# Second attention and expert half of a transformer block: new instruction orders, chunk 0 normalised by VectorE, group scores from pair sums, SP's tables ahead of the weights

## The reference

```
x = x + xattn0(LN(x), ctx)        # one head, softmax over 32 keys; out = (LN(x) + attended) @ Wo.T + bo
x = x + ffn0(LN(x))               # router, 8 experts, the best one per token; gelu MLP 128-256-128, times its gate
x = x + xattn1(LN(x), ctx, mask)  # 16 heads of width 8, 32 keys
x = x + ffn1(LN(x))               # 16 experts of width 96, top 4 of 16 out of the 2 best of 4 groups, plus a shared expert
```

```
scores = sigmoid(LN(x) @ gate_w.T);  sb = scores + gate_bias
group_scores = sum(top_2 of the 4 sb in each group)      # 4 groups of 4 experts
keep the 2 best groups; tidx = top_4 of the kept sb
w = scores[tidx] / (sum + 1e-20) * 2.5
y = sum over experts of combine[:, e] * (silu(g_e) * u_e) @ w2_e;   out = y + shared
```

## Time and profile before

| | us |
|---|---|
| median of three runs | 311.48 (310.99 to 311.97) |
| the profiled execution | 313.38 |
| its span, first to last instruction | 311.6 |
| TensorE busy in the span | 264.1 (85%) |
| VectorE busy | 191.7 (62%) |
| ScalarE busy | 162.9 (52%) |
| GpSimd busy | 155.4 (50%) |
| mean granted TensorE clock | 0.919 of full |

### The profile page before, as it was taken

How to read it: one execution, slowest core, us unless ns; L and a number is a source line. 1 busy time by engine, 2 the same in 40 slices (tenths; PEclk the granted TensorE clock), 3 DMA queues, 4 the chain that set the end, 5 groups by cost and what they waited for, 6 DMA issues and landing times. The chain is left out here.

```text
span 311.6 us, 4963 instructions
## 1 busy us (share of the span) xinstructions
PE 264.1 (85%) x1542; PEld 193.6 (62%) x1542; DVE 191.7 (62%) x577; ACT 162.9 (52%) x324; POOL 155.4 (50%) x182
## 2 busy tenths in 40 slices
PE   8899962259989287979899987999899989899993
PEld 7689852249984042444468645875477867687871
DVE  5555557014441348666975998689976599665561
ACT  2946330485641034157488654878457745455541
POOL 6722577439402888251176151743178535565561
PEclk9996655559999969999999999999999999999998
DMA  7960013447841111000000000000000000000000
GB/s 239 405 236 1 18 35 101 119 127 191 241 130 37 51 35 34 8 2 0 2 0 2 1 0 1 2 0 14 23 1 0 2 34 1 1 2 34 0 0 34
DMA packets 15372, 16.86 MB, mean 54 GB/s; under 512 B 2147, under 2 KB 13011, under 8 KB 15091
## 3 DMA queue, kind: packets, MB, share of 16 engines
q1 hardware_dynamic: 9520, 11.65, 11.8%
q10 hardware_dynamic: 4802, 2.80, 2.9%
q0 software_dynamic: 1024, 2.10, 2.4%
HBM read 11.96 MB, written 4.59 MB: 53 GB/s over the span
## 5 line engine op out<-in xcount | busy, mean ns | idle before, releaser
L854 POOL TENSOR_TENSOR lring<-hm,hring 128x512 fp32r<-128x512 f32 (+1 forms) x52 | 67.9, 1307 | 77.6 <-ACT hring L746 76.3
L740 ACT ACTIVATE act<-bank 128x512 f32<-128x512 f32 (+1 forms) x52 | 31.0, 597 | 38.5 <-PE bank L1166 38.3
L1143 DVE TENSOR_TENSOR act<-act,bank 128x512 f32<-128x512 f32 x48 | 32.9, 685 | 27.0 <-PE bank L1166 25.7
L1166 PE MATMUL bank<-xTh,gu1h 128*128 128x512 f32 (+1 forms) x104 | 43.6, 419 | 2.6 <-DVE hm L1154 1.7
L1166 PE MATMUL bank<-xTh,gu1l 128*128 128x512 f32 (+1 forms) x104 | 41.1, 395 | 0.0
L1166 PE MATMUL bank<-xTl,gu1h 128*128 128x512 f32 (+1 forms) x104 | 40.8, 393 | 0.0
L581 ACT ACTIVATE xn<-x,shift_of,rstd 128x128 f32<-128x128 f32 x64 | 26.4, 483 | 26.4 <-POOL shift_of L775 26.3
L1154 DVE TENSOR_TENSOR hm<-act,bank 128x512 f32<-128x512 f32 (+1 forms) x52 | 35.6, 685 | 7.4 <-PE bank L1166 4.9
L746 ACT CAST hring<-hm 128x512 fp32r<-128x512 f32 (+1 forms) x52 | 32.1, 618 | 12.4 <-DVE hm L1154 11.4
L1166 PEld LDWEIGHTS bank<-xTh,gu1h 128*128 128x128 f32 (+1 forms) x104 | 19.3, 186 | 14.8 <-DVE act L1143 3.6
L788 POOL DMA_INDIRECT xn<-sorted_y,home x16 | 15.7, 983 | 21.2 <-DMA sorted_y<-ys 17.3
(11 more groups left out here) (217 smaller groups left out, 521.0 us busy)
## 6 DMA issues: line engine op xcount, KB each, us to landing
w<-in_w SPq DMA_DIRECT2D x23, 129.0 KB, 2.4
wf<-in_gu SPq DMA_DIRECT2D x1, 1632.0 KB, 14.2
xs<-sorted_x SPq DMA_DIRECT2D x23, 64.0 KB, 2.5
sorted_y<-ys ACTq DMA_DIRECT2D x11, 128.0 KB, 3.1
x<-in_x SPq DMA_DIRECT2D x4, 256.0 KB, 5.1
w<-in_w SPq DMA_DIRECT2D x1, 1024.0 KB, 9.6
out_x<-x SPq DMA_DIRECT2D x4, 256.0 KB, 2.0
w<-in_w SPq DMA_DIRECT2D x1, 768.0 KB, 14.9
```

Of the source, the lines that this page charges most:

```text
L740: nc.scalar.activation(act[0:m, n % 4, :], bank[0][0:m, :], ACT.Silu).then_inc(s.act_ready1, 1)
L854: nc.gpsimd.tensor_tensor(lring[0:m, n % 4, :], hm[0:m, n % 4, :], hring[0:m, n % 4, :].bitcast(F32), ALU.subtract).then_inc(s.hml_ready, 1)
L1143: nc.vector.tensor_tensor(act[:, n % 4, :], act[:, n % 4, :], bank[1][:, :], ALU.mult).then_inc(s.prod_ready1, 1)
L1166: return nc.tensor.matmul(dst, lhsT, rhs, start=start, stop=stop, skip_group_check=True)
```

## The change

New lists for all four engines in both halves. The parts of them that matter most (old line with -, new with +; each is cut out of a longer list):

```diff
 ORDER0
-"DVE": ... shift:1 soft:1 add:0 shift:2 soft:2 add:1 shift:3 soft:3 pick:0 add:2 slot:0 pick:1 add:3 slot:1 ...
+"DVE": ... shift:1 soft:1 add:0 shift:2 soft:2 add:1 shift:3 pick:0 soft:3 slot:0 add:2 pick:1 add:3 slot:1 ...
-"POOL": rstd:0 wnorm:0 rstd:1 ... rstd2:0 rstd2:1 rstd2:2 scatter:0 scatter:1 scatter:2 rstd2:3 scatter:3 scatter:4 ...
+"POOL": rstd:0 rstd:1 wnorm:0 ... rstd2:0 rstd2:1 scatter:0 scatter:1 rstd2:2 scatter:2 scatter:3 rstd2:3 scatter:4 ...
-"PE": ... score:3 wturn:2 turn2:0 own:2 logit:0 mix:2 wturn:3 rank:0 turn2:1 own:3 logit:1 mix:3 rank:1 ...
+"PE": ... score:3 wturn:2 turn2:0 own:2 logit:0 mix:2 rank:0 turn2:1 wturn:3 logit:1 own:3 mix:3 rank:1 ...
 ORDER1
-"DVE": combine:0 combine:1 max:0 combine:2 div:0 combine:3 add:0 max:1 route0:0 ... route5:0 hm:0 div:1 prod:1 route6:0 route7:0 ...
+"DVE": combine:0 norm2:0 max:0 max:1 max:2 max:3 combine:1 stat2:1 combine:2 recip:0 recip:1 div:0 add:0 stat3:0 stat2:2 norm3:0
+       max:4 max:5 max:6 max:7 route0:0 ... route7:0 hm:0 recip:2 prod:1 hm:1 prod:2 recip:3 div:1 hm:2 prod:3 add:1 stat3:1 ...
-"POOL": fetch:0 ... fetch:6 rstd2:0 fetch:7 fetch:8 bias1:0 ... fetch:15 rstd2:3 rstd3:0 bias1:2 lowx:0 low:0 ...
+"POOL": fetch:0 ... fetch:5 rstd2:0 fetch:6 fetch:7 bias1:0 ... fetch:12 rstd2:1 rstd3:0 fetch:13 lowx:0 bias1:1 fetch:14 rstd2:2 fetch:15 low:0 ...
-"ACT": norm2:0 unturn2:0 qcopy:0 norm2:1 mcopy:0 exp:0 unturn2:1 norm2:2 qcopy:1 norm3:0 unturn3:0 round:0 mcopy:1 lgcopy:0 sg:0 exp:1 silu:0 ...
+"ACT": unturn2:0 qcopy:0 mcopy:0 exp:0 norm2:1 unturn2:1 qcopy:1 unturn3:0 lgcopy:0 sg:0 mcopy:1 round:0 exp:1 silu:0 ...
-"PE": ... score:1 turn3:0 mturn:1 logit:0 scoreT:1 g:0 u:0 zav:1 g:1 u:1 g:2 y:0 turn2:2 wo:1 q:2 gturn:0 ...
+"PE": ... score:1 turn3:0 logit:0 mturn:1 scoreT:1 g:0 u:0 zav:1 g:1 gturn:0 u:1 g:2 e:1 u:2 g:3 e:2 y:0 u:3 g:4 y:1 wo:1 ...
-"PE": ... zav:2 y:7 e:10 y:8 g:11 y:9 gturn:1 turn2:3 u:11 wo:2 ...
+"PE": ... zav:2 e:11 u:11 g:12 y:9 u:12 y:10 g:13 wo:2 u:13 e:12 turn2:3 g:14 gturn:1 ...
-"PE": ... zav:3 g:20 e:19 u:20 g:21 y:18 gturn:2 ...
+"PE": ... zav:3 g:22 u:22 y:19 e:22 g:23 y:20 u:23 e:23 y:21 g:24 y:22 u:24 wo:3 e:24 g:25 gturn:2 ...
-"PE": ... g:36 u:36 e:35 gturn:3 y:33 e:36 ...  e:50 g:51 y:48 u:51 e:51 y:49 y:50 y:51 oturn:3
+"PE": ... e:38 u:39 gturn:3 g:40 y:37 e:39 ...  e:50 g:51 u:51 e:51 y:48 y:49 y:50 y:51 oturn:3
```

Fewer fillers, and one weight load fewer ahead of the tokens, now behind both tables:

```diff
-LEAD0 = 5
+LEAD0 = 4
-FILL = {"q": 4, "score": 2, "mturn": 8, "scoreT": 2, "zav": 2, "wo": 13, "turn3": 14, "logit": 2}
+FILL = {"q": 1, "score": 2, "mturn": 7, "scoreT": 2, "zav": 2, "wo": 13, "turn3": 6, "logit": 1}
...
             _, experts = nc.values_load_multi_w_load_instructions(tile_e ...)
-            for t in range(LEAD0):
-                load_weights(t, experts[t])
             sp.wait_ge(s.table_ready, 2)
             _, first = nc.values_load_multi_w_load_instructions(tile_r ...)
+            for t in range(LEAD0):
+                load_weights(t, experts[t])
             sp.wait_ge(s.scattered, 16 * NT)
```

```diff
+                if k >= 2 and b == 0:
+                    nc.gpsimd.tensor_scalar(ve[:, own, :], mv[:, own, :, 1], EPS, None, ALU.add).then_inc(s.ln_step[k], 3)
+                    pool.wait_ge(s.ln_step[k], 3)
+                    nc.gpsimd.tensor_tensor(rstd[:, own, :], ve[:, own, :], mhalf[:, 0:TPB], ALU.pow).then_inc(s.ln_rstd[k], 1)
+                    return
...
+            def normalise_first(k):
+                own = ln(k, 0)
+                v.wait_ge(s.ln_rstd[k], 1)
+                for j in range(TPB):
+                    nc.vector.tensor_scalar(normal(k, 0)[:, j, :], x[:, j, :], mv[:, own, j, 0:1], rstd[:, own, j:j + 1],
+                                            ALU.subtract, ALU.mult).then_inc(s.xn_ready[k], 1)
```

```diff
+            def maxima(c, g):
+                ...
+                nc.vector.tensor_reduce(mpad[:, :, KV * g:KV * g + HG], bank[4 + g][:, :]..., AX, ALU.max).then_inc(s.mx1_ready, 1)
+            def invert(c, h):
+                v.wait_ge(s.av_mm, 2 * c + 1)
+                nc.vector.reciprocal(half(rz1, h), half(bank[4], h)).then_inc(s.rz1_ready, 1)
```

```diff
-                    nc.vector.tensor_tensor(large, pairs[:, :, 0], pairs[:, :, 1], ALU.max)
-                    step(nc.vector.tensor_tensor(small, pairs[:, :, 0], pairs[:, :, 1], ALU.min))
-                    nc.vector.tensor_tensor(g4[0], pr_t[:, 0, :, 0], pr_t[:, 0, :, 1], ALU.max)
-                    nc.vector.tensor_tensor(g4[1], pr_t[:, 0, :, 0], pr_t[:, 0, :, 1], ALU.min)
-                    step(nc.vector.tensor_tensor(g4[2], pr_t[:, 1, :, 0], pr_t[:, 1, :, 1], ALU.max))
-                    step(nc.vector.tensor_tensor(g4[3], g4[1], g4[2], ALU.max))
-                    step(nc.vector.tensor_tensor(gs[:, t, :].rearrange("p t g -> p (t g)"), g4[0], g4[3], ALU.add))
+                    nc.vector.tensor_tensor(sums[:, :, 0:3], four[:, :, 0:3], four[:, :, 1:4], ALU.add)
+                    nc.vector.tensor_tensor(sums[:, :, 3:5], four[:, :, 0:2], four[:, :, 2:4], ALU.add)
+                    step(nc.vector.tensor_tensor(sums[:, :, 5:6], four[:, :, 0:1], four[:, :, 3:4], ALU.add))
+                    step(nc.vector.tensor_reduce(gs[:, t, :].rearrange("p t g -> p (t g)"), sums, AX, ALU.max))
```

More of the change, by code:

```diff
@@ L51 @@
     "DVE": (
-        "moments:0 wnorm:0 bias:0 moments:1 wscale:0 moments:2 moments:3 value:0 shift:0 wT:0 route:0 soft:0 "
-        "shift:1 soft:1 add:0 shift:2 soft:2 add:1 shift:3 soft:3 pick:0 add:2 slot:0 pick:1 add:3 slot:1 "
-        "pick:2 slot:2 pick:3 slot:3 "
+        "moments:0 moments:1 bias:0 wnorm:0 moments:2 value:0 wscale:0 moments:3 wT:0 shift:0 soft:0 route:0 "
+        "shift:1 soft:1 add:0 shift:2 soft:2 add:1 shift:3 pick:0 soft:3 slot:0 add:2 pick:1 add:3 slot:1 pick:2 "
+        "slot:2 pick:3 slot:3 "
     ),
     "POOL": (
-        "rstd:0 wnorm:0 rstd:1 rstd:2 rstd:3 rstd2:0 rstd2:1 rstd2:2 scatter:0 scatter:1 scatter:2 rstd2:3 "
-        "scatter:3 scatter:4 scatter:5 scatter:6 scatter:7 scatter:8 scatter:9 scatter:10 scatter:11 "
-        "scatter:12 scatter:13 scatter:14 scatter:15 "
+        "rstd:0 rstd:1 wnorm:0 rstd:2 rstd:3 rstd2:0 rstd2:1 scatter:0 scatter:1 rstd2:2 scatter:2 scatter:3 "
+        "rstd2:3 scatter:4 scatter:5 scatter:6 scatter:7 scatter:8 scatter:9 scatter:10 scatter:11 scatter:12 "
+        "scatter:13 scatter:14 scatter:15 "
     ),
     "ACT": (
-        "tri:0 norm:0 kv:0 kv:1 unturn:0 fold:0 norm:1 norm:2 exp:0 unturn:1 norm:3 wcopy:0 exp:1 unturn:2 "
-        "wcopy:1 exp:2 unturn:3 norm2:0 wcopy:2 unturn2:0 exp:3 norm2:1 wcopy:3 pexp:0 unturn2:1 norm2:2 "
-        "pexp:1 unturn2:2 norm2:3 pexp:2 unturn2:3 pexp:3 "
+        "kv:0 norm:0 fold:0 kv:1 unturn:0 norm:1 unturn:1 exp:0 norm:2 wcopy:0 exp:1 unturn:2 norm:3 tri:0 "
+        "wcopy:1 exp:2 unturn:3 norm2:0 unturn2:0 exp:3 wcopy:2 norm2:1 pexp:0 unturn2:1 wcopy:3 pexp:1 norm2:2 "
+        "unturn2:2 norm2:3 pexp:2 unturn2:3 pexp:3 "
     ),
     "PE": (
[3 rows of a table removed]
[3 rows of a table added]
     ),
@@ L221, in xattn_moe_kernel @@
         ra, rb, rc, rd = (sb(f"route{i}", [P, NT, E1]) for i in range(4))
[L222 to L223 removed]
+        pair = sb("pair", [P, NT * NG, 6])
         gs = sb("gs", [P, NT, NG])
@@ L1029, in combine, with half @@
                     v.wait_ge(s.x2_ready, TPB * (b + 1))
-                    statistics(2, b)
-            def maxima(c):
-                v.wait_ge(s.s1_mm, c + 1)
-                if c:
-                    v.wait_ge(s.mt_mm, c)
-                for g in range(HG):
-                    last = nc.vector.tensor_reduce(mpad[:, :, KV * g:KV * g + HG],
-                                                   bank[4 + g][:, :].rearrange("p (j i k) -> p j i k", j=TPB, i=HG), AX, ALU.max)
-                last.then_inc(s.mx1_ready, 1)
-            def divide(c):
-                half = [slice(h * CH // 2, (h + 1) * CH // 2) for h in range(2)]
-                v.wait_ge(s.av_mm, 2 * c + 1)
-                for h in range(2):
-                    last = nc.vector.reciprocal(rz1[:, half[h]], bank[4][:, half[h]])
-                step(last)
+            def maxima(c, g):
+                if g == 0:
+                    v.wait_ge(s.s1_mm, c + 1)
+                    if c:
+                        v.wait_ge(s.mt_mm, c)
+                nc.vector.tensor_reduce(mpad[:, :, KV * g:KV * g + HG], bank[4 + g][:, :].rearrange("p (j i k) -> p j i k", j=TPB, i=HG),
+                                        AX, ALU.max).then_inc(s.mx1_ready, 1)
+            def half(buf, h):
+                return buf[:, h * CH // 2:(h + 1) * CH // 2]
+            def invert(c, h):
+                v.wait_ge(s.av_mm, 2 * c + 1)
+                nc.vector.reciprocal(half(rz1, h), half(bank[4], h)).then_inc(s.rz1_ready, 1)
+            def divide(c):
                 v.wait_ge(s.av_mm, 2 * c + 2)
@@ L1127, in stage1 @@
                     combine(n)
+                elif stage == "stat2":
+                    statistics(2, n)
```

(6 more changed lines are left out.)

19 lines of the change are left out of this document (10 added, 9 removed), and 90 rows, old and new, of tables (ORDER0, ORDER1).

## The result

The changed kernel took 318.0 us (median of 4 runs, 317.05 to 318.7) against 311.24 us (4 runs, 310.53 to 311.97) for the kernel before on the same chip: ratio 1.0215, interval 1.0176 to 1.0254. The forecast was 301.7 us, and 318 lies far outside its range of 296.5 to 308. The profiled execution took 317.57 us (span 315.7 us). Executions of one kernel on one chip spread by 3 to 4%, with stretches at half the TensorE clock at other places each time, so all ratios here are of the fast ones of each kernel, those within 1.5% of its fastest.

A forecast was written before the change was run, and what follows sets the result against it. It took short-step chains to bound the kernel to 109 us, near-serial attention to 144 us, then TensorE's matmuls plus waits. Terms -1.5 - 3.1 - 1.1 - 3.4 - 0.7 = -9.8 us took 311.48 to 301.7 us; eight-in-ten range 296.5 to 308.

The forecast's parts named there:

- Front: Scatters to first tiles: new orders and earlier table reads bring scatters and token load forward, first gelu bound by casts; -1.5 us.
- Chunk 0 normalised by VectorE: Second attention's layernorm: earlier power, four VectorE tensor_scalars and fewer fillers bring q closer to the moments; -3.1 us.
- The second rival: Both new VectorE normalisations are each held for one GpSimd instruction of 0.95 us; +1.9 us, 303.6 us, chance 0.13.
- The tail of this, from q to the softmax, ... keeps its durations: Chunk 0 from q through softmax and reciprocals to wo:0: stages are split but no unready work added, so durations stay.
- From wo:0 to the first block: Stretch before the expert blocks: add:0 follows at once and normalisation shortens, against a later round:0; -1.1 us.
- The blocks: Expert blocks: waits for division and gates go, the hm wait halves, pair sums give 0, new waits cost 1.0 us; -3.4 us.
- The tail: End of the kernel: y:48 moves behind e:51, so u:51 and what follows come earlier; -0.7 us.
- The first: Rival: new head-of-line waits in four queues eat the blocks' 3.4 us and the front gives nothing; 306.6 us, chance 0.22.
- The fourth: Rival: thirteen fillers removed leave TensorE's clock at 0.5 in chunk 0 until the blocks; +3.2 us net, 314.7 us, chance 0.04.

The follow-up runs named there:

- e5: The changed kernel unchanged, run again on another chip; ratio 1.004 against the kernel before.
- e6: The changed kernel with GpSimd subtracting only 64 of 512 columns of each hidden block's low part from block 5 on; ratio 0.9632 against the kernel before.
- e8: e4 with five places in its orders changed, moving wo, gturn, q:3 and y:48 stages; ratio 1.0086 against the kernel before.
- e2: The changed kernel with the second half's orders of the kernel before, keeping the fewer fillers; ratio 0.9926 against the kernel before.
- e4: The changed kernel with both the second half's orders and the fillers of the kernel before; ratio 0.9885 against the kernel before.
- e10: e4 with each of GpSimd's low subtractions made as two instructions of 256 columns; ratio 0.9983 against the kernel before.
- e16: The same kernel as e4, run again on another chip; ratio 1.0 against the kernel before.
- e3: The changed kernel with the number of filler matmuls of the kernel before (47 instead of 34); ratio 0.9944 against the kernel before.

## Why the prediction was wrong, point by point

The forecast had the profile 9.8 us shorter, and it is 4.2 us longer. Of these 14.0 us, 8.1 lie from the first block to the end (forecast 4.1 us gained, with the tail; 4.0 lost) and 6.4 between the first fetch and the first block (4.2 gained; 2.2 lost); the front gave 0.5 us more than forecast.

**Front: right, as far as one profile can say.** Predicted -1.5 us; the first fetch comes 2.0 us earlier (98.51 to 96.55). The size is partly luck: kernels with the same front on the same chip have their first fetch up to 6.5 us apart (96.15, 91.42 and 89.68 us in e5, e6 and e8), and e1, the front alone, gained 0.45% with an interval that reaches 1. The moments that carried the argument did come as predicted. The first token load is issued at 60.13 us (61.3 predicted), and the first gelu starts at 66.78 us (66.5), bound by ScalarE's casts:

```profile
62.15 1.75 ACT L661 CAST w2h<-w 128x384 fp32r<-128x384 f32 x4
...
65.49 1.28 ACT L684 ACT_TABLE_LOAD   x1
66.78 1.14 ACT L684 ACTIVATE hT<-bank,w 128x128 f32<-128x128 f32 x4
```

**Chunk 0 normalised by VectorE: right to q.** Four operations in 1.33 us, from 105.61 us, 0.04 us after the power ends; q starts 4.09 us after the moments instead of 6.73, a gain of 2.6 us (3.1 predicted), and 4.7 us earlier in all.

```profile
105.61 1.33 DVE L1065 TENSOR_SCALAR xn<-x,mv,rstd 128x128 f32<-128x128 f32 x4 [1.55 <-POOL rstd L775]
```
```profile
104.52 1.05 POOL L775 TENSOR_TENSOR rstd<-ve,mhalf 128x4 f32<-128x4 f32 x1
105.76 1.15 POOL L795 DMA_INDIRECT xn<-sorted_y,home  x1 [0.19 <-issue]
```

The second rival's collision came, but small. In every profile with this part the fetch beside the four takes 1.15 us instead of 0.95, and the last of the four ends 0.02 us after it and takes 0.56 us instead of 0.34: 0.2 us, not 0.95. At the changed kernel's second normalisation the last takes 0.42 us. In the old second orders (e2, e4, e8, e10, e16) GpSimd's bias addition stands beside that one, and its first operation takes 1.28 us: there the hold has the rival's size, from a tensor instruction.

**"The tail of this, from q to the softmax, ... keeps its durations": wrong.** Here the 4.7 us were lost again. The scores ran at the half clock (2.3 us from first to last where it had been 1.3), the maximum waited 3.4 us behind the run of fetches, which was new, since the new GpSimd order has rstd2:1 behind fetch:12 and the old one had it in between; and scoreT ran mostly at the half clock (3.6 us from its start to the first exponential instead of 2.1). I had priced what each queue does, not what stands on GpSimd while VectorE waits for a semaphore. Where the wait is missing (e5), the time from first fetch to first block is 4.9 us shorter, about these 3.4 us and scoreT's 1.5. The first block starts at 144.07 us, 0.2 us later than before.

**From wo:0 to the first block:** -1.1 us predicted, -0.7 measured (13.05 to 12.39 us). The term is borne out in sign and roughly in size.

**The blocks: the step that failed most.** I wrote that the pair sums of the routing are "0.3 us for a chunk of an engine that isn't the bound: 0", had the wait for hm fall by 0.6 us, as the last chunk's routing is spread between products, and charged 1.0 us for new waits. The waits that I said would go did go: those for the division wholly (3.5 us), that of gturn:3 from 1.1 to 0.5 us. The new ones are 8.6 us: 6.8 more for hm and act (9.8 instead of 3.0), and 1.8 for gturn:0, which the new order has ahead of u:1. The price of one held operation stood in the earlier trace rows (0.17 to 1.25 us), and I used it only for the normalisation. The right question was how many of the routing's small operations the new order puts beside GpSimd's tensor instructions: 19 instead of 6, 12 us more of held time, 4.4 us more of TensorE's idle time than the old orders have with the rest of the change (e16). The pair sums aren't to blame: e4 has them too, and 7 held operations (e16 has 8). So the term was -3.4 us and measured +4.4 (from the first block's g to g:51). A small slip besides: for wo:2 my own terms give 4.9 - 4.4 = 0.5 us, not 0.8; no such wait shows. The Trainium skill, "SBUF — State Buffer", section "Who interferes with whom", says that a VectorE instruction with two SBUF inputs contends with a GpSimd instruction that reads SBUF. The trace agrees for the routing's operations (1.28 us instead of 0.19), and the products with one input in PSUM keep their 0.68 us; I had read that section for the fetch, where 0.2 us came of it, and not for the subtractions, where it decides.

**The tail: right.** -0.7 us predicted, -0.5 measured. From g:51's first matmul to the end it is 11.34 us before (and in e16) and 10.87 after: u:51 starts 0.78 instead of 1.40 us behind g:51, and from there to the end it takes 0.15 us more. The waits ahead of the last matmuls fall from 1.7 to 1.0 us.

**The rivals.** The first comes nearest in kind: new waits at the heads of the queues ate the 3.4 us. But the blocks lost 4.4 us on top, which no rival had. The fourth named the low clock in chunk 0 and put it down to missing fillers. The clock did fall, but behind the wait of 4.2 us; on chips without that wait (e5, e6) the fewer fillers seem to bring 1.2 to 1.6 us against e3 (42.62 and 42.24 against 43.84 us, on different chips), and no half-clock stretch lies between the scores' end and the first block. So its cause isn't borne out.

## What to carry to other kernels

Before moving small VectorE operations in time, list what GpSimd runs beside them: here each one between SBUF tiles (reductions excepted) lasted as long as what was left of the GpSimd tensor instruction beside it, and back-to-back GpSimd work held one after another. An order that packs four queues more tightly can lose more by this than it gains in waits, so price it by count: held operations times the GpSimd duration is the VectorE time at stake (here 12 us more), of which TensorE saw about a third. And measure a change of one or two per cent on more than one chip: this one cost 2.15%, 1.5% and 0.4% on three occasions, the last not told from none.

## What the runs showed that I had not expected

- On three of five occasions, VectorE's first maximum came late behind a run of GpSimd's fetches (2.14 to 2.18 us after the start of the last of five, five profiles; 0.6 to 1.6 us late behind three, three profiles), on two it didn't. The same three show SP's and ScalarE's queues slow beside the scatters: seven zero writes take 7.98 us in the changed kernel's first profile (7.40 in the earlier trace rows), and eight take 3.88 us in e5:

```profile
49.83 7.98 ACTq L650 DMA_DIRECT2D sorted_x<-zeros  x7
```
```profile
53.69 3.88 ACTq L650 DMA_DIRECT2D sorted_x<-zeros  x8
```

 That both come of GpSimd's indirect transfers is argued from their falling together, not shown; why it shows on one chip and not on another stays open. The Trainium skill, "SBUF — State Buffer", section "Who interferes with whom", says that a tensor_reduce on trn2 never contends with GpSimd: its duration here agrees (0.68 us in every case), its start does not tell, since it is the start that is late.
- VectorE's small tensor_scalars, with one tensor input, are held by GpSimd's tensor instructions too: one of 128x4 takes 0.90 us instead of 0.17 (221.29 us in the changed kernel).
- GpSimd's subtraction costs its kernel far more than its own queue shows: with 64 columns instead of 512 (0.33 us instead of 1.30) the changed kernel is 4.1% faster, though TensorE waited only 1.0 us for its output.
